# Rounding the first and third matrix of a routed expert on GpSimd instead of loading their rounded copies

## The chip, the cores and the metric

The kernel runs on one core of one Trainium2 chip. The metric is the device time of one execution, in microseconds (us), as a median of several runs.

## The reference

The reference is a small network on 2048 tokens of width 512: a mixture of four experts chosen by token id, a feed-forward block with Hadamard rotations, a WKV recurrence, and last a routed mixture of experts. Only the last part matters here:

```
scores = softmax(xf @ gate_w);  sel = top_k(scores + expert_bias, 2)
routed_in = xf[token_idx] * top_scores_sorted[:, None]        # sorted by expert
h = silu(ragged_dot(routed_in, w1, counts)) * ragged_dot(routed_in, w3, counts)
routed_out = ragged_dot(h, w2, counts)
out = silu(xf @ sw1) * (xf @ sw3) @ sw2                       # shared expert
out = out.at[token_idx].add(routed_out)
```

There are eight routed experts. Each has w1 and w3 of 512 x 448 and w2 of 448 x 512. With the inputs of the reference the experts get 275, 166, 897, 2048, 311, 197, 202 and 0 rows.

## The kernel before, in words

Each float32 product is made of three products of rounded numbers (type float32r): the low part of the activation with the high part of the weight, high with low, and high with high. So each weight matrix must stand in SBUF twice: as Wh, its rounded copy, and as Wl, the raw weight minus Wh.

The work of the last layer goes in tiles of 128 rows, numbered t. Tiles 0 to 15 belong to the shared expert and tiles 16 to 54 to the routed ones. With 128 rows to a tile and at least one tile for each expert, routed expert e0 has tiles 16 to 18, e1 19 and 20, e2 21 to 28, e3 29 to 44, e4 45 to 47, e5 48 and 49, e6 50 and 51, and e7 52 to 54 (it has no rows, and the tiles that are left fall to it).

TensorE takes the routed tiles in one fixed order, in the loop behind L1298. In each turn it transposes the input of tile t+1 (`d_x`, L1282), makes the two up products of tile t (`d_up`, L1311, 24 matmuls), transposes the hidden rows of tile t-1 (`d_mid`, L1330), and makes the down product of tile t-2 (`d_down`, L1346, 12 matmuls). `d_up` of an expert's first tile waits on `s_w13` for both parts of its w1 and w3; `d_down` waits on `s_w2`.

The weights lie in two slots, and expert e uses slot e mod 2. GpSimd (POOL) fills them, with `w_all(idx, slot, ups, downs)`, where idx is e+1. It works in program order:

- It waits until TensorE has done the last up product that reads the slot (`s_dup` at `ups`), which is that of the last tile of expert e-2.
- `w_high` (L585) starts a DMA that casts a raw matrix from HBM straight into Wh. It is issued for w1 (p = 0) and w3 (p = 1), one behind the other.
- `w_low` (L592) waits for the raw matrix in the staging buffer `wst[p]` and for Wh, subtracts one from the other into Wl, and waits for its own end.
- `w_raw` (L576) starts the load of the next expert's raw matrix into `wst[p]`, which is free then.
- Then it waits for the last down product that reads the slot (`s_dd` at `downs`), and does the same for w2 (p = 2).

`alone` (L572) is an addition of one column on GpSimd, put ahead of many of these instructions for every idx above 2. The pair of calls at L742 and L743 runs twice in a hardware loop (experts e2 to e5), and two more calls follow behind it. Expert e0 (idx 1) is loaded by other code that the change leaves as it is.

Ahead of the routed tiles GpSimd issues 32 scatters (L732) of the sorted rows to DRAM. SyncE (SP) waits for their landing and then loads the tiles' inputs into `xsd` (L479, `load`), stores each tile's result (L483, `store`), and fetches the shared expert's rows into `row` (L503). VectorE adds those rows to `xres` on every second tile (L1877), which has two inputs in SBUF. At the end GpSimd gathers the routed results (L754 and L761), VectorE adds them, and SyncE writes the output.

Of the kernel before, what the change touches and what calls it, by code (L numbers as in the profile page):

```python
# [4 lines left out]
ALU = mybir.AluOpType  # L5
# [7 lines left out]
D = 512  # L13
# [29 lines left out]
HID = 448  # L43
# [28 lines left out]
def program(nc, x, tok, ctx, g_xattn, g_ffn, su_ug, su_dp, wscale_ug, wscale_dp, w_up, w_gate, w_down,  # L72
            wkv_w, wkv_u, gate_w, w1, w2, w3, sw1, sw2, sw3, expert_bias, consts, out):
    es = ExitStack()
    with es:
        def sem(name):
            return es.enter_context(nc.semaphore(name))
# [11 lines left out]
        def keep(name, shape, dt=F32):  # L89
            t = nc.alloc_sbuf_tensor_at(name, shape, dt, offset=top[0])  # L90
            size = 4
            for n in shape[1:]:
                size *= n
            top[0] += (size + 31) // 32 * 32
            return t
# [5 lines left out]
        slot = keep("slot", [P, TT], I32)  # L101
# [93 lines left out]
        Wh, Wl = W[:, :, 0, :], W[:, :, 1, :]  # L195
# [117 lines left out]

        s_wst = [sem(f"s_wst{i}") for i in range(3)]
        s_whi = [sem(f"s_whi{i}") for i in range(3)]
        s_w13 = sem("s_w13")
        s_w2 = sem("s_w2")
        s_dxn = sem("s_dxn")
# [4 lines left out]
        s_dup = sem("s_dup")  # L323
# [5 lines left out]
        s_dd = sem("s_dd")  # L329
# [37 lines left out]
        def f32(ap):  # L367
            return ap.bitcast(F32)
# [8 lines left out]
        def w_rows(p, width, at=None):  # L377
            q, step = ((P, G_W), (P, HID), (HP, D))[p]
            return wst[p if at is None else at][0:q, 0:HC * step].rearrange("p (k n) -> p k n", k=HC)[:, :, 0:width]
# [135 lines left out]
        def _(pool):  # L515
# [42 lines left out]
            def w_part(idx, p):  # L558

                if isinstance(idx, int) and idx == 0:  # L560
                    return shared_part[p]
                w, q = ((w1, P), (w3, P), (w2, HP))[p]
                return w[bass.ds(idx - 1, 1), :, :].rearrange("e (k p) n -> p (e k) n", p=q)
# [3 lines left out]
            def alone(idx):  # L567


                if not isinstance(idx, int) or idx > 2:  # L570
                    n = places[0] = places[0] + 1
                    pool.tensor_tensor(pace[:, n:n + 1], pace[:, 0:1], pace[:, 0:1], ALU.add)  # L572

            def w_raw(idx, p):

                pool.dma_start(w_rows(p, (HID, HID, D)[p]), w_part(idx, p)).then_inc(s_wst[p], 16)  # L576

            def w_place(whole, slot, p, width):

                q, at, step = ((P, W_1, G_W), (P, W_3, HID), (HP, W_2, D))[p]  # L580
                return whole[0:q, slot, at:at + HC * step].rearrange("p (k n) -> p k n", k=HC)[:, :, 0:width]

            def w_high(idx, p, slot):

                pool.dma_start(w_place(Wh, slot, p, (HID, HID, D)[p]), w_part(idx, p)).then_inc(s_whi[p], 16)  # L585

            def w_low(idx, p, slot):

                width = (HID, HID, D)[p]
                pool.wait_ge(s_wst[p], 16 * idx)  # L590
                pool.wait_ge(s_whi[p], 16 * (idx + 1))
                pool.tensor_tensor(w_place(Wl, slot, p, width), w_rows(p, width), f32(w_place(Wh, slot, p, width)), ALU.subtract)\  # L592
                    .then_inc((s_w13, s_w13, s_w2)[p], 1)
                if p < 2:
                    pool.wait_ge(s_w13, 2 * idx + p + 1)
                else:
                    pool.wait_ge(s_w2, idx + 1)
# [26 lines left out]
                else:  # L624
                    pool.wait_ge(s_w2, 1)

            def w_all(idx, slot, ups=None, downs=None, more=True):


                if ups is not None:  # L630
                    pool.wait_ge(s_dup, ups)
                    alone(idx)
                for p in range(2):
                    w_high(idx, p, slot)
                for p in range(2):
                    w_low(idx, p, slot)
                    if more:
                        alone(idx)
                        w_raw(idx + 1, p)
                if downs is not None:  # L640
                    pool.wait_ge(s_dd, downs)
                    alone(idx)
                w_high(idx, 2, slot)
                w_low(idx, 2, slot)
                if more:
                    alone(idx)
                    w_raw(idx + 1, 2)
# [80 lines left out]
            for t in range(TT):  # L728
                for k in range(2):
# [3 lines left out]
                                            rows_at[n % 8], None).then_inc(s_rsc[n % 8], 16)  # L733

            w_all(2, 1, TT, TT)

            def w_next(idx, slot, more=True):
                last = pool.value_load(tend1_i[0:1, bass.ds(idx - 3, 1)], min_val=1, max_val=NT1)
                w_all(idx, slot, last + TT, last + TT, more)
# [1199 lines left out]
```

## Time and profile before

| | us |
|---|---|
| median of 3 runs | 1395.21 |
| lowest and highest | 1388.55 and 1401.52 |
| the profiled execution | 1396.1 |
| its span, first to last instruction | 1394.4 |

The mean granted clock of TensorE in the profiled execution is 0.959 of full speed. Instants below are microseconds from the start of the span. In rows of instructions, "x8" counts instructions, and the bracket is the idle time of the engine ahead of them with what ended it.

### The profile page before, as it was taken

What the parts mean: (1) busy time and instruction counts of PE and PEld (TensorE: products, weight loads), DVE (VectorE), ACT (ScalarE), POOL (GpSimd) and SP (SyncE); (2) the same over time, 40 slices, a digit from 0 to 9 for tenths busy, and PEclk for the clock granted to TensorE, in tenths of its full rate; (3) what the DMA queues carried; (4) which work ended last, traced back from release to release, by engine and by line L of the source; (5) the groups of instructions that cost most, each with busy time, mean ns of one, the idle gap of its engine ahead of it and who ended that gap; (6) DMA issues with size and microseconds to landing.
All of it is one profiled execution on the core that took longest, in us unless ns stands there. A gap on an engine that the chain in (4) does not pass through costs nothing.

```text
span 1394.4 us, 18292 instructions
## 1 busy us (share of the span) xinstructions
PE 1271.6 (91%) x6256; PEld 1073.6 (77%) x6257; DVE 652.2 (47%) x1103; ACT 446.7 (32%) x755; POOL 391.7 (28%) x327
## 2 busy tenths in 40 slices
PE   4999899999999999999999889995899999998670
PEld 3888778887888888888888778884788888887560
DVE  6555356644366646674555575563123222222116
ACT  3333342333245323531343457421122222221110
POOL 2221111000022302221334231446454310035554
PEclk9999999999999999999999999998899999999785
DMA  6821456544669845965964030435777552257647
GB/s 204 263 84 54 145 210 243 211 159 191 246 216 349 302 181 202 366 239 196 310 226 156 26 84 31 155 117 206 198 222 230 168 141 75 75 181 220 167 145 254
DMA packets 99035, 259.69 MB, mean 186 GB/s; under 512 B 8636, under 2 KB 42648, under 8 KB 86680
## 3 DMA queue, kind: packets, MB, share of 16 engines
q1 hardware_dynamic: 64824, 160.19, 32.4%
q0 software_dynamic: 33680, 98.35, 23.4%
q8 instruction: 41, 0.67, 0.2%
q10 hardware_dynamic: 464, 0.27, 0.1%
q14 instruction: 26, 0.21, 0.0%
HBM read 183.02 MB, written 75.76 MB: 186 GB/s over the span
## 4 chain that ended last, share of the span: by engine, by line
PE 63%; issue 14%; POOL 10%; DMA 7%; DVE 4%; another core or an unknown queue 1%; ACT 1%; POOLq 0%; ACTq 0%; DVEq 0%
PE bank L1145 25%; PE bank L1173 12%; POOL W L592 6%; PE bank L1311 6%; DMA W<-in_L_ffn_w 5%; PE bank L1070 4%; PE bank L1090 4%; PE bank L1346 2%; PE bank L1100 2%; POOL xs_sorted L732 2%; POOL fin_high L761 1%; PE bank L1117 1%; PE bank L1112 1%; DMA wdn<-in_L_ffn_W_down 1%
## 5 line engine op out<-in xcount | busy, mean ns | idle before, releaser
L1145 PE MATMUL bank<-xTh,G 128*128 128x512 f32 x1024 | 279.4, 398 | 1.8 <-DVE xTl L1592 1.8
L1145 PEld LDWEIGHTS bank<-xTh,G 128*128 128x128 f32 x1024 | 189.4, 189 | 42.8 <-issue 3.4
L1311 PE MATMUL bank<-W,dxh 128*128 (+2 forms) x880 | 204.9, 376 | 0.0
L1311 PEld LDWEIGHTS bank<-W,dxh 128*128 128x128 f32 x880 | 171.8, 195 | 15.9
L1173 PE MATMUL bank<-DN,bhh 128*128 128x512 f32 x512 | 157.9, 390 | 0.0
L1311 PE MATMUL bank<-W,dxl 128*128 (+2 forms) x440 | 117.4, 390 | 32.4 <-POOL W L592 16.4
L1145 PE MATMUL bank<-xTl,G 128*128 128x512 f32 x512 | 138.1, 392 | 0.0
L1746 DVE TENSOR_TENSOR dmid<-bank,dsg 128x448 f32<-128x448 f32 x55 | 34.3, 623 | 203.0 <-ACT dsg L954 194.7
L592 POOL TENSOR_TENSOR W<-wst,W 128x1792 fp32r<-128x1792 f32 (+1 forms) x24 | 101.4, 4226 | 87.7 <-DMA W<-in_L_ffn_w 86.3
L1614 DVE SCALAR_TENSOR_TENSOR bs<-bank,tab,bs 128x512 f32<-128x512 f32 x64 | 47.5, 743 | 160.8 <-PE bank L1145 160.8
L1346 PE MATMUL bank<-W,dhh 112*128 (+1 forms) x440 | 114.6, 403 | 0.0
L1311 PEld LDWEIGHTS bank<-W,dxl 128*128 128x128 f32 x440 | 82.5, 197 | 41.3 <-issue 33.8
L1145 PEld LDWEIGHTS bank<-xTl,G 128*128 128x128 f32 x512 | 96.7, 189 | 20.9
L1173 PEld LDWEIGHTS bank<-DN,bhh 128*128 128x128 f32 x512 | 96.2, 188 | 21.3 <-issue 1.7
L954 ACT ACTIVATE dsg<-bank 128x448 f32<-128x448 f32 x55 | 29.9, 544 | 244.0 <-PE bank L1311 235.2
L1173 PE MATMUL bank<-DN,bhl 128*128 128x512 f32 x256 | 103.8, 405 | 0.0
L1346 PEld LDWEIGHTS bank<-W,dhh 112*128 112x128 f32 x440 | 85.3, 194 | 20.4
L842 ACT ACTIVATE bhh<-bs 128x512 fp32r<-128x512 f32 x64 | 40.3, 629 | 185.4 <-DVE bs L1614 185.4
L1738 DVE TENSOR_TENSOR dxl<-bank,dxh 128x512 fp32r<-128x512 f32 x55 | 37.9, 688 | 115.8 <-ACT dxh L936 115.8
L836 ACT ACTIVATE bs<-bank,tab 128x512 f32<-128x512 f32 x64 | 44.1, 689 | 137.7 <-PE bank L1145 137.7
L522 POOL TENSOR_TENSOR rstd<-vare,cst 128x4 f32<-128x4 f32 x12 | 12.4, 1031 | 228.9 <-DVE vare L1507 228.9
L964 ACT ACTIVATE dys<-bank 128x512 f32<-128x512 f32 x55 | 32.9, 598 | 125.1 <-PE bank L1346 104.0
(247 smaller groups left out, 1961.6 us busy)
## 6 DMA issues: line engine op xcount, KB each, us to landing
G<-gate_up_split SPq DMA_DIRECT2D x48, 1024.0 KB, 7.0
DN<-down_split SPq DMA_DIRECT2D x24, 1024.0 KB, 5.0
wst<-in_L_ffn_w POOLq DMA_DIRECT2D x24, 896.0 KB, 6.2
W<-in_L_ffn_w POOLq DMA_DIRECT2D x24, 896.0 KB, 7.6
gate_up_split<-G SPq DMA_DIRECT2D x16, 1024.0 KB
y_all<-dys SPq DMA_DIRECT2D x55, 256.0 KB
xs_sorted<-zero POOLq DMA_DIRECT2D x3, 3328.0 KB, 21.1
xsd<-xs_sorted SPq DMA_DIRECT2D x39, 256.0 KB, 3.3
```

The lines of the kernel that those rows point to most:

```text
L592: pool.tensor_tensor(w_place(Wl, slot, p, width), w_rows(p, width), f32(w_place(Wh, slot, p, width)), ALU.subtract)\
L836: act.activation(bs[g % 2][:, :], bank[0][:, :], ACT.Silu, scale=tab[:, T_WGT + g % NK:T_WGT + g % NK + 1]).then_inc(s_bs, 1)
L842: act.activation(bhh[g % 2][:, :], bs[g % 2][:, :], ACT.Copy).then_inc(s_bhh, 1)
L1070: mm = pe.matmul(bank[2 + t % 2][:, :], a[t % 2][:, k, :], w[:, bass.ds(ex * DC + k, 1), :], start=(n == 0), stop=(n == 3 * DC - 1))
L1090: mm = pe.matmul(bank[4 + t % 2][:, :], a[t % 2][:, k, :], w[:, bass.ds(ey * DC + k, 1), :], start=(n == 0), stop=(n == 3 * DC - 1))
L1145: mm = pe.matmul(bank[m][:, :], G[:, c % 2, f, h, m, i, :], a[b % 2][:, i, :], start=(n == 0), stop=(n == 3 * DC - 1))
L1173: mm = pe.matmul(bank[2 + i][:, :], a[g % 2][:, i * P:(i + 1) * P], DN[:, c % 2, f, h, :], start=(k == 0 and n == 0), stop=(k == NK - 1 an ...
L1311: mm = pe.matmul(bank[o][:, 0:width], a[par][:, k, :], w[:, bass.ds(slot, 1), at + k * step:at + k * step + width].rearrange("p a n -> p ( ...
L1346: mm = pe.matmul(bank[4][:, :], a[par][:, k, :], w[0:HP, bass.ds(slot, 1), W_2 + k * D:W_2 + (k + 1) * D].rearrange("p a n -> p (a n)"), s ...
L1614: dve.scalar_tensor_tensor(out=bs[g % 2][:, :], in0=bank[1][:, :], scalar=tab[:, T_WUP + g % NK:T_WUP + g % NK + 1], in1=bs[g % 2][:, :], ...
L1738: dve.tensor_tensor(dxl[t % 2][:, :, :].rearrange("p k n -> p (k n)"), bank[0][:, :], f32(dxh[t % 2][:, :, :]).rearrange("p k n -> p (k n) ...
L1746: dve.tensor_tensor(dmid[t % 2][:, :], bank[3][:, 0:HID], dsg[:, :], ALU.mult).then_inc(s_dmid, 1)
```

## The change

GpSimd makes the rounded copies of w1 and w2 itself. For the experts from e1 on, `w_cut` waits for the raw matrix in `wst[p]`, runs one `alone`, copies the matrix with `tensor_copy` into Wh (float32 to float32r), and waits for the copy's end on a new semaphore, `s_wcut`. `w_low_of` is `w_low` without the two waits ahead. `w_all` now takes the order: DMA of w3's rounded copy; copy of w1, subtraction of w1, load of the next raw w1; subtraction of w3, load of the next raw w3; wait for the down products; copy of w2, subtraction of w2, load of the next raw w2. The same holds for all seven calls of `w_all`.

```diff
+            def w_cut(idx, p, slot):
+                width = (HID, HID, D)[p]
+                pool.wait_ge(s_wst[p], 16 * idx)
+                alone(idx)
+                pool.tensor_copy(w_place(Wh, slot, p, width), w_rows(p, width)).then_inc(s_wcut, 1)
+                pool.wait_ge(s_wcut, 2 * idx - 3 + p // 2)
+
+            def w_low_of(idx, p, slot):
+                width = (HID, HID, D)[p]
+                pool.tensor_tensor(w_place(Wl, slot, p, width), w_rows(p, width), f32(w_place(Wh, slot, p, width)), ALU.subtract)\
+                    .then_inc((s_w13, s_w13, s_w2)[p], 1)
+                if p < 2:
+                    pool.wait_ge(s_w13, 2 * idx + p + 1)
+                else:
+                    pool.wait_ge(s_w2, idx + 1)
+
+            def w_all(idx, slot, ups, downs, more=True):
+                pool.wait_ge(s_dup, ups)
+                alone(idx)
+                w_high(idx, 1, slot)
+                w_cut(idx, 0, slot)
+                w_low_of(idx, 0, slot)
+                if more:
                     alone(idx)
-                for p in range(2):
-                    w_high(idx, p, slot)
-                for p in range(2):
-                    w_low(idx, p, slot)
-                    if more:
-                        alone(idx)
-                        w_raw(idx + 1, p)
-                if downs is not None:
-                    pool.wait_ge(s_dd, downs)
+                    w_raw(idx + 1, 0)
+                w_low(idx, 1, slot)
+                if more:
                     alone(idx)
-                w_high(idx, 2, slot)
-                w_low(idx, 2, slot)
+                    w_raw(idx + 1, 1)
+                pool.wait_ge(s_dd, downs)
+                alone(idx)
+                w_cut(idx, 2, slot)
+                w_low_of(idx, 2, slot)
                 if more:
                     alone(idx)
                     w_raw(idx + 1, 2)
```

## Rows read from the trace of the kernel before

**Rows 1.** The page, part 1: busy time, share and instructions of each engine.

```profile
PE 1271.6 (91%) x6256; PEld 1073.6 (77%) x6257; DVE 652.2 (47%) x1103; ACT 446.7 (32%) x755; POOL 391.7 (28%) x327
```

**Rows 2.** Windows of the routed tiles: us, busy per engine, clock, DMA share, GB/s.

```profile
964.00:979.00 15.00, 0.97 (x5) 0.48 (x5) 0.00 (x0) 0.60 (x1) 8.83 (x9) 0.69 0.83 269
...
1128.00:1233.00 105.00, 105.00 (x541) 92.51 (x540) 26.94 (x42) 25.48 (x49) 1.52 (x3) 1.00 0.27 86
...
1300.00:1327.00 27.00, 15.95 (x70) 13.66 (x69) 3.13 (x5) 3.16 (x7) 15.21 (x9) 0.75 0.61 155
```

**Rows 3.** Waits of PE from 960 on: us, times, longest.

```profile
PE bank L1311 <- POOL W L592: 16.4, 2, 11.0
PE bank L1282 <- issue: 14.0, 1, 14.0
```

**Rows 4.** Timeline of PE around tiles 49 to 52.

```profile
1271.09 0.60 PE L1282 MATMUL bank<-cst,xsd 128*128 128x128 f32 x4
...
1279.66 0.60 PE L1282 MATMUL bank<-cst,xsd 128*128 128x128 f32 x4
1285.65 1.85 PE L1311 MATMUL bank<-W,dxl 128*128 x4 [5.39 <-POOL W L592]
...
1316.30 1.86 PE L1311 MATMUL bank<-W,dxl 128*128 x4 [11.05 <-POOL W L592]
```

**Rows 5.** Timeline of POOL while it loads e5, e6 and e7.

```profile
1253.41 0.18 POOL L572 TENSOR_TENSOR pace<-pace 128x1 f32<-128x1 f32 x1 [3.12 <-PE bank L1346]
...
1268.02 0.19 POOL L572 TENSOR_TENSOR pace<-pace 128x1 f32<-128x1 f32 x1
1268.70 1.53 POOL L585 DMA_DIRECT2D W<-in_L_ffn_w  x2 [0.49 <-issue]
1275.95 4.05 POOL L592 TENSOR_TENSOR W<-wst,W 128x1792 fp32r<-128x1792 f32 x1 [5.72 <-DMA W<-in_L_ffn_w]
...
1281.48 3.97 POOL L592 TENSOR_TENSOR W<-wst,W 128x1792 fp32r<-128x1792 f32 x1
...
1294.63 4.63 POOL L592 TENSOR_TENSOR W<-wst,W 112x2048 fp32r<-112x2048 f32 x1 [7.30 <-DMA W<-in_L_ffn_w]
...
1300.21 0.21 POOL L572 TENSOR_TENSOR pace<-pace 128x1 f32<-128x1 f32 x1
```

**Rows 6.** Groups of POOL by form: count, busy us, mean ns, idle before.

```profile
L592 POOL TENSOR_TENSOR W<-wst,W 128x1792 fp32r<-128x1792 f32 x16 | 64.5, 4034 | 36.1 <-DMA W<-in_L_ffn_w 34.7 <-DMA wst<-in_L_ffn_w 1.1
L592 POOL TENSOR_TENSOR W<-wst,W 112x2048 fp32r<-112x2048 f32 x8 | 36.9, 4610 | 51.7 <-DMA W<-in_L_ffn_w 51.6
...
L661 POOL TENSOR_SCALAR ce<-cd,wlim 128x512 f32<-128x512 f32 x16 | 25.1, 1570 | 103.7 <-DVE cd L1639 102.8 <-POOL W L592 0.9
...
L669 POOL TENSOR_TENSOR cev<-cnum,ce 128x512 f32<-128x512 f32 x14 | 18.1, 1296 | 35.6 <-issue 27.3 <-DVE ce L1658 8.3
...
L528 POOL TENSOR_TENSOR nmr<-negm,rstd 128x4 f32<-128x4 f32 x8 | 1.6, 203 | 0.6
...
L517 POOL MEMSET zero<- 128x128 f32 x1 | 0.2, 205 | 3.0 <-DMA cst<-shape_constants 3.0
L700 POOL MEMSET pace<- 128x32 f32 x1 | 0.1, 125 | 0.0
```

**Rows 7.** Instructions on xsd: landing of the loads issued at 972, then of all.

```profile
DMA to landing us min/median/max: 6.6/7.2/7.8
...
DMA to landing us min/median/max: 2.6/3.3/7.8
```

**Rows 8.** Timeline of PE: input of tile 18, eight up matmuls of tile 17 and of tile 18.

```profile
992.21 0.65 PE L1282 MATMUL bank<-cst,xsd 128*128 128x128 f32 x4 [2.45 <-DMA xsd<-xs_sorted]
...
994.51 2.97 PE L1311 MATMUL bank<-W,dxh 128*128 x8
...
1002.41 1.79 PE L1311 MATMUL bank<-W,dxh 128*128 x8
```

**Rows 9.** L1877 on VectorE, durations from 1000 on, min/median/max.

```profile
L1877 DVE SCALAR_TENSOR_TENSOR xres<-row,gates,xres x16: 742/744/3871, 1016.9 to 1278.3; 128x512 f32<-128x512 f32 x16
```

More of the change, by code:

```diff
@@ L315, in program @@
         s_whi = [sem(f"s_whi{i}") for i in range(3)]
+        s_wcut = sem("s_wcut")
         s_w13 = sem("s_w13")
@@ L625, in shared_low @@
                     pool.wait_ge(s_w2, 1)
-            def w_all(idx, slot, ups=None, downs=None, more=True):
-                if ups is not None:
-                    pool.wait_ge(s_dup, ups)
-                    alone(idx)
-                for p in range(2):
-                    w_high(idx, p, slot)
-                for p in range(2):
-                    w_low(idx, p, slot)
-                    if more:
-                        alone(idx)
-                        w_raw(idx + 1, p)
-                if downs is not None:
-                    pool.wait_ge(s_dd, downs)
-                    alone(idx)
-                w_high(idx, 2, slot)
-                w_low(idx, 2, slot)
+            def w_cut(idx, p, slot):
[19 more added lines that the diff above has]
+                if more:
+                    alone(idx)
+                    w_raw(idx + 1, 0)
+                w_low(idx, 1, slot)
+                if more:
+                    alone(idx)
+                    w_raw(idx + 1, 1)
[3 more added lines that the diff above has]
+                w_low_of(idx, 2, slot)
                 if more:
```

## The prediction

> **What bounds the kernel now.** I read the page first. TensorE is busy for 91% of the span [rows 1], so a change off TensorE can only win what TensorE loses to waits. The change touches the routed tiles alone, so the windows of that stage come next. Between 1128 and 1233 us, while e3's 16 tiles run, TensorE is busy for all 105 us at full clock and GpSimd for 1.5 us [rows 2]: nothing about the weights is worth anything there. From 1300 to 1327 it is busy for only 16 of 27 us, at 0.75 of the clock, and GpSimd for 15 [rows 2]. The list of TensorE's waits gives the price: two waits on the subtractions of L592, 16.4 us in all, and one of 14.0 us ahead of tile 16's transposes [rows 3]. The timeline puts the two: 5.39 us ahead of tile 50, the first of e6, and 11.05 us ahead of tile 52, the first of e7 [rows 4]. e5 and e6 have two tiles each, and a tile takes 1279.66 - 1271.09 = 8.57 us [rows 4], while GpSimd takes 1300.21 - 1268.02 = 32.2 us for one expert [rows 5]. That is the bound here: GpSimd's round per expert against 17.1 us of tiles.
>
> In GpSimd's round for e6, 5.72 us go in a wait for the two cast DMAs and 7.30 us in the wait for w2's [rows 5]. Over the run, L592 stands idle 34.7 + 51.6 us for such DMAs [rows 6], but only the rounds of e6 and e7 are on the path.
>
> **What a copy costs.** The trace has no `tensor_copy` on GpSimd, so I bound it per column. The product of L669 takes 1.296 us for 512 columns and that of L528 0.203 us for 4, which is 2.15 ns a column over some 0.2 us; L592 gives (4.034 - 0.203) / 1788 = 2.14 [rows 6]. So the rate holds to 1792 columns, and writing float32r costs nothing extra. That is two reads and one write. A memset, one write, rises from 0.125 us at 32 columns to 0.205 at 128: 0.83 ns a column [rows 6]. A copy has one read and one write. By the memset it would take 1.7 us for w1 and 1.9 us for w2; by L592 4.0 and 4.6 us. The dearest row with one large input is L661, 2.69 ns a column [rows 6], which gives 5.0 and 5.7 us. I take 1.2 ns, nearer the memset, since one read and one write can overlap where two reads seem to add: C = 2.3 us for w1 and D = 2.7 us for w2. The ends 1.7/1.9 and 5.0/5.7 go into the range.
>
> The Trainium skill, GPSIMD Engine Reference, section Engine selection, says that on GpSimd an operation with one input runs at roughly line rate, where one with two inputs is about twice as slow as VectorE. At its 1.2 GHz that would be an estimate of 1.5 us for 1792 columns over the fixed cost, near the lower end; L661, with one large input at 2.69 ns a column [rows 6], speaks against reading the rule for every such operation. By the rule the sum would win some 1 us more.
>
> **GpSimd's round, new.** From its start (the wait on the slot's last up product passed) to w3's subtraction done:
> - first pace instruction to the DMA's issue 0.7, one issue of the pair's 1.53, so 0.77 [rows 5]; second pace and gaps 0.6
> - the copy C, its own wait 0.1
> - subtraction of w1 4.05; to the next subtraction 1281.48 - 1280.00 = 1.5 (a pace and a raw load); subtraction of w3 4.0 [rows 5].
> That is 11.8 + C = 14.1 us, against 17.4 now (1268.02 to 1285.45) [rows 5]. For e7 nothing more is loaded, so 1.4 goes: 10.4 + C = 12.7. The w2 part, from the last down product that reads the slot: two paces and gaps 0.9, D, 0.1, 4.6, so 5.6 + D = 8.3 us. The load of the next raw w2 ends it with 1.2 (1299.26 to 1300.21 is 0.95, and where the loop turns it is more) [rows 5]. Issues, paces and waits are counted in these, and every one of them is on GpSimd's own path.
>
> **The chain at the end.** In the unshifted clock of the trace:
> - e5's w2 may start at 1253.4, after tile 44's down product [rows 5]: done 1261.7, raw load issued 1262.9. Tile 47's up product is long done.
> - e6's w3 is done at 1262.9 + 14.1 = 1277.0. TensorE wants it at 1280.1, just after the transposes of 1279.66 [rows 4]. The wait of 5.39 goes, and so do some 2 us of half clock behind it.
> - Raw load until 1278.2. Now e6's w2 is late by something new: slot 1 is read by tile 47's down product until 1279.7 [rows 4]. Then w2 is done at 1288.0, the raw load at 1289.2.
> - e7's w3 is done at 1289.2 + 12.7 = 1301.9. TensorE is ready for tile 52 at 1280.1 + 2 x 8.57 = 1297.2, and so still waits, 4.7 us. In short, tile 52 starts at 1296.9 + C + D.
> Now it starts at 1316.30 [rows 4]. So the tail wins 14.4 us. What follows (three tiles, the gathers, the additions, the output) hangs on TensorE and moves with it. The copies themselves cost nothing before e6: those of e1 to e5 lie under tiles that run without a gap [rows 2]. Closest is e2: its round begins after tile 18 and tile 21 comes some 20.8 us later, against 14.1 needed.
>
> With L592's rate for the copies GpSimd no longer waits for tile 47, and tile 52 starts at 1290.4 + 2C + 2D = 1307.6: 8.7 us won. With L661's rate it is 1311.8: 4.5 won. With the memset's it is 1300.5: 15.8 won.
>
> **The start of the stage.** Two cast DMAs are issued right behind the scatters, and the inputs of tiles 16 and 17 are loaded at 972, behind them. They land after 6.6 and 7.8 us; the median of all such loads is 3.3 [rows 7]. TensorE waits 14.0 us there [rows 3], with the DMA engines 83% busy at 269 GB/s [rows 2]. One of the two DMAs, 0.92 MB, goes: at 269 GB/s that is at most 3.4 us; I take 2. Tile 18's input makes TensorE wait 2.45 us, and the eight matmuls behind take 2.97 us in place of 1.79 [rows 8]. The cast DMA of w2, which the code puts in the same stretch, goes as well. That is worth 0 to 4; I take 1. From there TensorE and the waits of GpSimd on it move together, so these 3 us (0 to 7) reach the end.
>
> **Sum.** 14.4 + 3 = 17.4 us off the profiled execution's 1396.1 (span 1394.4 and 1.7 around it) gives 1378.7. That execution lies 0.9 above the median, so my forecast for the median is 1378.
>
> **The rivals.**
> - The copy runs at the rate of L592 or L661. For it: L661 has one large input and is dearer than a product with two [rows 6]. Against it: a scalar from memory is part of L661. The gain is 8.7 + 3 or 4.5 + 3, and the time 1384 to 1388.
> - The gain is given back through VectorE. L1877 takes 742 ns, but up to 3871 [rows 9], which is about when a subtraction of GpSimd runs; SyncE waits for it before it fetches the next input. GpSimd's reading time per expert rises from 12.7 to 17.7 us, and some of the 16 additions meet it. If three more do and each holds TensorE up by 1.2 us, and the start wins nothing, 11 us are left: 1384. The Trainium skill, SBUF — State Buffer, section Who interferes with whom, states that a VectorE instruction with two SBUF inputs contends with a GpSimd instruction that reads SBUF, and that the second waits for the first to end; the trace's 3871 ns agrees. By it the copy is a new holder, while the cast DMA never was one.
> - w3's DMA ends last. In e7's round its subtraction could start 8.7 us in. The DMA is issued at 0.7, and e6's first one is there 1275.95 - 1268.70 = 7.25 us after its issue [rows 5]: at 8.0, with 0.7 to spare. Each us more costs one; at 3 us more the time is 1380.
> - Slower: rounding is software on GpSimd, and the copy costs more than any row. Tile 52 starts later than now once 1290.4 + 2C + 2D passes 1316.3, that is from 3.3 ns a column on. At 4.5 ns (8.3 and 9.4 us) it starts at 1325.8, 9.5 later; with the 3 us won at the start the time is 1402. Against it: the subtraction rounds too, at no price [rows 6].
>
> **How the numbers follow.** A measurement of this kernel tells about 1% from no change. That bound lies at 1381.3 below and 1409 above. The forecast has 0.62 and its own times run from 1373 to 1383, most of it under the bound; the copy at the dearer rates 0.20; VectorE or w3's DMA together 0.12; slower than before 0.06, little of that over 1409. Faster by over 1%: 0.55. Within 1%: 0.42. Slower by over 1%: 0.03. The range is 1371 (the memset's rate and the start's full 7 us) to 1388 (L661's rate).
>
> **What would show it.** Right: `tensor_copy` on GpSimd at 2 to 3 us; TensorE's waits on the subtractions down from two to one of some 5 us, ahead of tile 52; no wait ahead of tile 50; GpSimd waiting for tile 47's down product in e6's round; its waits on W's DMA gone but for moments; the 14.0 us ahead of tile 16 down to 12. The forecast is wrong if the copies take 4 us or more, if tile 52 still starts over 10 us late, or if xsd waits grow.

## The result and the profile after

The changed kernel takes 1375.12 us, the median of 4 runs (1371.3 to 1377.29), against 1393.39 us for the kernel before (4 runs). The medians lie 18.3 us apart; the ratio of the two, as the comparison estimates it, is 0.9857 with a 95% interval of 0.9821 to 0.9893, which is 19.9 us. On another chip, beside other runs, the same two kernels gave 1371.77 and 1385.98 us, ratio 0.9898 (0.9882 to 0.9915), 14.1 us. The forecast was 17.4, and 1378 us for the median.

The page of the changed kernel, part 1, answers to [rows 1]. GpSimd is busier by 15 us and has 12 more instructions: the copies add 25.1 us, and 14 issues of a DMA at some 0.77 us each are gone:

```profile
PE 1265.0 (92%) x6256; PEld 1069.8 (78%) x6257; DVE 652.6 (48%) x1103; ACT 446.4 (33%) x755; POOL 407.0 (30%) x339
```

TensorE's waits from 960 us on answer to [rows 3]. Of 16.4 us in two waits on the subtractions, 3.7 in one are left, and the wait ahead of tile 16 is 12.2 in place of 14.0:

```profile
PE bank L1300 <- issue: 12.2, 1, 12.2
PE bank L1364 <- issue: 5.4, 1, 5.4
PE bank L1329 <- POOL W L593: 3.7, 1, 3.7
PE bank L1300 <- DMA xsd<-xs_sorted: 2.2, 4, 1.3
```

The groups of GpSimd by form answer to [rows 6]: count, busy us, mean ns, then the idle time before. The copies are there as CAST, seven of each size, at 1.694 and 1.888 us. The subtraction of w3, which alone still waits for a casting DMA, has 5.8 us of idle time left; [rows 6] had 34.7 and 51.6:

```profile
L593 POOL TENSOR_TENSOR W<-wst,W 128x1792 fp32r<-128x1792 f32 x9 | 36.3, 4033 | 7.1 <-DMA W<-in_L_ffn_w 5.8 <-DMA wst<-in_L_ffn_w 1.3
...
L638 POOL TENSOR_TENSOR W<-wst,W 112x2048 fp32r<-112x2048 f32 x7 | 33.1, 4726 | 0.6
...
L633 POOL CAST W<-wst 112x2048 fp32r<-112x2048 f32 x7 | 13.2, 1888 | 0.5 <-PE bank L1364 0.5
...
L633 POOL CAST W<-wst 128x1792 fp32r<-128x1792 f32 x7 | 11.9, 1694 | 0.0
```

The timeline of GpSimd from the start of e6's round answers to [rows 5]:

```profile
1249.93 0.20 POOL L573 TENSOR_TENSOR pace<-pace 128x1 f32<-128x1 f32 x1
1250.27 0.77 POOL L586 DMA_DIRECT2D W<-in_L_ffn_w  x1
...
1251.19 1.69 POOL L633 CAST W<-wst 128x1792 fp32r<-128x1792 f32 x1
1252.96 4.06 POOL L638 TENSOR_TENSOR W<-wst,W 128x1792 fp32r<-128x1792 f32 x1
...
1260.09 4.00 POOL L593 TENSOR_TENSOR W<-wst,W 128x1792 fp32r<-128x1792 f32 x1 [2.07 <-DMA W<-in_L_ffn_w]
...
1272.84 0.33 POOL L573 TENSOR_TENSOR pace<-pace 128x1 f32<-128x1 f32 x2 [7.77 <-PE bank L1364]
1273.11 1.89 POOL L633 CAST W<-wst 112x2048 fp32r<-112x2048 f32 x1
...
1279.91 0.74 POOL L577 DMA_DIRECT2D wst<-in_L_ffn_w  x1
...
1280.88 0.77 POOL L586 DMA_DIRECT2D W<-in_L_ffn_w  x1
...
1290.34 3.96 POOL L593 TENSOR_TENSOR W<-wst,W 128x1792 fp32r<-128x1792 f32 x1 [2.70 <-DMA W<-in_L_ffn_w]
```

The wait of 7.77 us for tile 47's down product is the new link that the prediction named. From there to the end of e7's w3, GpSimd needs 1294.30 - 1272.84 = 21.5 us, 2.70 of them a wait for w3's own DMA. The timeline of TensorE answers to [rows 4]:

```profile
1250.12 1.06 PE L1329 MATMUL bank<-W,dxl 128*128 x4
...
1259.81 0.65 PE L1300 MATMUL bank<-cst,xsd 128*128 128x128 f32 x4 [1.31 <-DMA xsd<-xs_sorted]
1261.71 1.85 PE L1329 MATMUL bank<-W,dxl 128*128 x4 [1.25 <-issue]
1263.37 3.19 PE L1329 MATMUL bank<-W,dxh 128*128 x8
...
1272.94 1.06 PE L1329 MATMUL bank<-W,dxl 128*128 x4
...
1294.50 1.54 PE L1329 MATMUL bank<-W,dxl 128*128 x4 [3.71 <-POOL W L593]
```

Tile 50 (1272.94) no longer waits for weights. But tile 49 starts 1261.71 - 1250.12 = 11.6 us after tile 48 in place of 8.57. The transposes of tile 50's input waited 1.31 us for its load, the product behind them 1.25 more, and then eight matmuls took 3.19 us in place of 1.79. Tile 50 follows after 11.2 us. That is 3.0 + 2.7 = 5.7 us that the forecast did not have. A window over that stretch gives the granted clock, the third value from the right:

```profile
1261.70:1267.00 5.30, 5.29 (x14) 4.73 (x15) 0.12 (x1) 0.00 (x0) 3.29 (x3) 0.50 0.52 169
```

It is 0.50, the lower of TensorE's two levels (1.2 and 2.4 GHz), and it fell after the idle 1.31 and 1.25 us.

**Where the 22.3 us between the two profiled spans lie.** I measured every run from the end of the last scatter, where the first changed instruction stands, and cut what follows at the starts of tiles 19 and 52 (first product of `d_up`). All columns are differences of instants in the timelines, in us. The last column is the part of "19 to 52" that lies between the starts of tiles 48 and 52; four tiles without any wait would take 4 x 8.57 = 34.3 us.

```
run                    last scatter ends   to tile 19   19 to 52   52 to the end    48 to 52
before                 970.35              39.7         306.2      78.1             53.4
before, again          962.92              35.5         310.0      77.9             53.6
changed                964.35              35.4         294.7      77.6             44.4
changed, again         961.95              36.8         297.3      76.9             42.4
e1 w1 only             959.97              40.4         299.6      77.0             48.2
e2 w2 only             964.55              38.1         299.0      76.5             45.4
e3 all three           963.91              32.9         287.4      77.6             37.1
e3 again               965.07              32.0         287.5      77.8             37.1
e4 copy twice          962.81              37.6         290.4      77.2             40.9
e5 first round old     961.81              38.2         294.2      77.5             38.7
e6 DMAs kept           962.69              35.3         299.4      76.8             45.1
e7 raw w2 behind       964.31              36.8         293.8      76.8             41.9
e8 up weights first    970.17              31.9         284.1      76.1             34.3
e9 input first         968.95              35.1         288.2      77.5             39.0
```

Of the 22.3 us, 6.0 lie ahead of anything changed, 4.3 before tile 19, 11.5 between tiles 19 and 52, and 0.5 behind. The first 6.0 are chance: the kernel before, profiled again, ends its scatters at 962.92, and a changed one (e8) at 970.17. Of the 11.5 us between tiles 19 and 52, 9.0 lie between tiles 48 and 52. The other 2.5 lie between tiles 19 and 48, where TensorE waits for no weights in either kernel; that stretch takes from 249.2 to 256.4 us over the fourteen profiles, and the second profile of the kernel before has the longest.

### The profile page after: what moved, and what is told of

Same layout as the page of the kernel before. It is cut to its first block, busy times and chain, and to the rows that moved or that the text cites. A ratio compares the mean times of both kernels' runs of the same rounds, so it can differ in the third digit from the quotient of the medians.

```text
span 1372.1 us, 18291 instructions
## 1 busy us (share of the span) xinstructions
PE 1265.0 (92%) x6256; PEld 1069.8 (78%) x6257; DVE 652.6 (48%) x1103; ACT 446.4 (33%) x755; POOL 407.0 (30%) x339
## 4 chain that ended last, share of the span: by engine, by line
PE 84%; DVE 4%; DMA 4%; issue 3%; POOL 2%; ACT 1%; another core or an unknown queue 1%; SPq 0%; ACTq 0%; POOLq 0%; DVEq 0%
PE bank L1163 26%; PE bank L1329 18%; PE bank L1191 12%; PE bank L1364 10%; PE bank L1088 4%; PE bank L1108 4%; PE bank L1118 2%; PE bank L1300 2%; PE bank L1348 1%; DMA xsd<-xs_sorted 1%; PE bank L1135 1%; DMA fin_high<-y_all,slr 1%; PE bank L1074 1%; DVE wl L1504 1%
## 5 line engine op out<-in xcount | busy, mean ns | idle before, releaser
L1329 PE MATMUL bank<-W,dxh 128*128 (+2 forms) x880 | 202.1, 372 | 0.0
L1329 PEld LDWEIGHTS bank<-W,dxh 128*128 128x128 f32 x880 | 169.0, 192 | 15.4
L1329 PE MATMUL bank<-W,dxl 128*128 (+2 forms) x440 | 115.1, 384 | 19.9 <-DVE dmid L1764 9.1
L1764 DVE TENSOR_TENSOR dmid<-bank,dsg 128x448 f32<-128x448 f32 x55 | 34.3, 624 | 186.6 <-ACT dsg L972 186.6
L1163 PEld LDWEIGHTS bank<-xTl,G 128*128 128x128 f32 x512 | 96.1, 188 | 20.8
L982 ACT ACTIVATE dys<-bank 128x512 f32<-128x512 f32 x55 | 32.9, 598 | 123.0 <-PE bank L1364 105.9
L1364 PE MATMUL bank<-W,dhl 112*128 (+1 forms) x220 | 66.2, 423 | 6.3 <-issue 5.4
## 6 DMA issues: line engine op xcount, KB each, us to landing
xs_sorted<-zero POOLq DMA_DIRECT2D x3, 3328.0 KB, 20.8
```

The costliest lines, as they stand in the source:

```text
L982: act.activation(dys[t % 2][:, :], bank[4][:, :], ACT.Copy).then_inc(s_dy, 1)
L1163: mm = pe.matmul(bank[m][:, :], G[:, c % 2, f, h, m, i, :], a[b % 2][:, i, :], start=(n == 0), stop=(n == 3 * DC - 1))
L1329: mm = pe.matmul(bank[o][:, 0:width], a[par][:, k, :], w[:, bass.ds(slot, 1), at + k * step:at + k * step + width].rearrange("p a n -> p ( ...
L1364: mm = pe.matmul(bank[4][:, :], a[par][:, k, :], w[0:HP, bass.ds(slot, 1), W_2 + k * D:W_2 + (k + 1) * D].rearrange("p a n -> p (a n)"), s ...
L1764: dve.tensor_tensor(dmid[t % 2][:, :], bank[3][:, 0:HID], dsg[:, :], ALU.mult).then_inc(s_dmid, 1)
```

## The experiments

**The kernel before and the changed one, once more.** No edit.

> The kernel before, profiled again on this chip. In its first profile the last scatter ended at 970.35 us, where every later profile has it at 960 to 964, though nothing ahead of it is changed; and the stage behind it took 424.05 us. If that shift is chance, the last scatter ends at 960 to 966 here. Tile 19 at 38 to 40 us after it, the stage at 422 to 425 us, two waits on the subtractions of 5 to 6 and 11 us.

The kernel before gave a ratio of 0.9999 (0.9977 to 1.0021) to itself. Its two waits on the subtractions are 5.56 and 11.44 us, so the tail of the stage is steady (53.4 and 53.6 us between tiles 48 and 52); 19 to 52 took 310.0 us. The start is not: tile 19 comes after 35.5 us, 4.2 earlier than in the first profile, with the same three casting DMAs.

> The changed kernel itself, beside the others on one chip. In its profile the input of tile 50 took 8.3 us to land, while the raw w2 and the rounded w3 were in flight. If that is the rule, TensorE again waits on xsd shortly before tile 49's products; if it was chance of the phase, the wait is absent and tile 52 starts some 3 to 6 us earlier after the last scatter than the 330.1 us of the first profile. Ratio to the kernel before 0.984 to 0.988.

The wait on xsd ahead of tile 49 came again, 1.14 us and 1.06 behind it, and the half clock too. Tile 52 starts at 334.1 us after the scatters, later than in the first profile and not earlier, and the ratio, 0.9898, lies just outside what I expected. So the late input was not a chance of one execution: both profiles of this kernel have it. It does not come every time either, as the profile of e5 shows.

**e1: round only w1 on GpSimd.** The copy of w2 goes back to its casting DMA:

```diff
-                w_cut(idx, 2, slot)
-                w_low_of(idx, 2, slot)
+                w_high(idx, 2, slot)
+                w_low(idx, 2, slot)
```

> Only w1 is rounded on GpSimd; the rounded copies of w2 and w3 are loaded by casting DMAs. Theory (GpSimd's round is the price): from tile 47's down product to e6's w2 done takes 12 to 13 us as in the kernel before, not the 6.9 of the changed kernel, so tile 52 starts some 6 us later than in the changed kernel, and the time is about 1381. Rival (only the DMA traffic counts, and w2's DMA runs while nothing else is in flight): no later than the changed kernel by more than 2 us, 1375 to 1377.

1379.5 us, ratio 0.9935 (0.9909 to 0.996). The timeline of GpSimd shows w2 of e6 and w3 of e7:

```profile
1271.30 0.72 POOL L586 DMA_DIRECT2D W<-in_L_ffn_w  x1
1280.57 4.61 POOL L593 TENSOR_TENSOR W<-wst,W 112x2048 fp32r<-112x2048 f32 x1 [8.55 <-DMA W<-in_L_ffn_w]
...
1295.84 3.95 POOL L593 TENSOR_TENSOR W<-wst,W 128x1792 fp32r<-128x1792 f32 x1 [2.66 <-DMA W<-in_L_ffn_w]
```

w2's part takes 13.9 us, 1271.30 to 1285.18, where I expected 12 to 13, and tile 52 waits 12.56 us. GpSimd starts that part 2.6 us after tile 47's down product is done, held by its own work alone, and tile 52 comes 31.3 us after that product, against 21.8 and 21.2 in the two profiles of the changed kernel: later by 9.5 us or more, where I expected 6. GpSimd's round is the price, as the theory has it. The changed kernel was not run on the chip of e1 to e4, so they are compared with it by their ratios. That of 0.9935 stands against 0.9857 and 0.9898, so w2's copy is worth between a third and somewhat over a half of the gain.

**e2: round only w2 on GpSimd.** w1 and w3 come by a pair of casting DMAs again, as in the kernel before.

> Only w2 is rounded on GpSimd; w1 and w3 come by a pair of casting DMAs. Theory (GpSimd's round): e7's round to the end of w3's subtraction takes 15.9 us as before in place of 13.7, so tile 52 starts 2 to 3 us later than in the changed kernel, and the start of the stage loses part of its 4 us, since two casting DMAs run beside the first inputs again: about 1380. Rival (the wait for w3's own DMA is what ends last, so w1's copy brings nothing at e7): tile 52 not later by more than 1 us and the time within 1 us of the changed kernel where the start is left out.

1379.32 us, ratio 0.9927 (0.9906 to 0.9948). In e7's round the pair's first DMA makes the subtraction wait 6.55 us, tile 52 waits 8.04 us, and 19 to 52 takes 3.0 us more than the changed kernel's mean of 296.0. Tile 52 comes 26.5 us after tile 47's down product, some 5 us later than in the changed kernel, where the theory had 2 to 3; its direction holds, its size was too small, and the rival falls. The copies alone bring 0.65% (e1) and 0.73% (e2), and the two together 1.4% in one comparison and 1.0% in the other. By the first the gains add up, by the second they overlap; these runs do not decide it.

**e3: round all three.** No casting DMA is left in the seven rounds.

```diff
-                w_high(idx, 1, slot)
                 w_cut(idx, 0, slot)
                 w_low_of(idx, 0, slot)
...
-                w_low(idx, 1, slot)
+                w_cut(idx, 1, slot)
+                w_low_of(idx, 1, slot)
```

> GpSimd rounds w3 too, so no casting DMA is left in these rounds. Theory (w3's DMA both ends last in the rounds of e6 and e7 and, beside the raw load of w2, makes the input of tile 50 late by 8.3 us from issue): e7's round to w3 done falls from 13.7 to about 12.2 us, the wait on xsd ahead of tile 49's products and the half clock behind it go (5.7 us), and the time is about 1368. Rival (VectorE's addition or chance made that input late): the wait on xsd stays, and the time is 1373 to 1375. Second rival (GpSimd's longer reading time collides with VectorE's additions): waits on xsd grow, 1377 or more.

1362.05 us, ratio 0.9799 (0.9777 to 0.9822): 25.7 us below the kernel before on that chip by the medians, 27.9 by the ratio, and 6 us below what the theory had. In TensorE's waits there is no wait on xsd at all:

```profile
PE bank L1300 <- issue: 10.7, 1, 10.7
PE bank L1329 <- POOL W L638: 2.6, 1, 2.6
PE bank L1329 <- DVE dmid L1764: 1.8, 2, 1.1
```

Tiles 19 to 52 take 287.4 us, 8.6 below the changed kernel's mean (6.3 of them between tiles 48 and 52), and tile 19 comes 3 us earlier. GpSimd's added reading time did not show: L1895, the addition of VectorE, was held up to 3.9 us here, as long as before [rows 9], and TensorE waited for nothing behind it.

**e4: every copy twice.** The second copy writes the same bytes.

```diff
-                pool.tensor_copy(w_place(Wh, slot, p, width), w_rows(p, width)).then_inc(s_wcut, 1)
-                pool.wait_ge(s_wcut, 2 * idx - 3 + p // 2)
+                for again in range(2):
+                    if again:
+                        alone(idx)
+                    pool.tensor_copy(w_place(Wh, slot, p, width), w_rows(p, width)).then_inc(s_wcut, 1)
+                    pool.wait_ge(s_wcut, 4 * idx - 7 + 2 * (p // 2) + again)
```

> Each copy of w1 and w2 is made twice, with a wait and one pace instruction between, so each w_cut is longer by 2.1 us. Theory (w3's DMA ends last in e7's round and hides w1's copy): only w2's second copy shows, tile 52 starts about 2 us later after tile 47's down product, and the time is about 1377. Rival (the sum of the prediction, tile 52 at a fixed time plus both copies): about 4 us later, 1379.

1368.68 us, ratio 0.9852 (0.9832 to 0.9872): no slower than the changed kernel, and 19 to 52 is shorter, 290.4 us. Both expectations missed this. The timelines show two effects. From tile 47's down product to tile 52 it takes 23.9 us against 21.8 and 21.2, so 2.1 to 2.7 more, which is near the theory's 2 and not the rival's 4. (GpSimd does not wait for that product here; it comes to w2 half a us after it, held by its own work.) But GpSimd issues the raw w2 only 0.4 us ahead of the load of tile 50's input and the cast of w3 1.1 us behind it, where the changed kernel issues them 2.2 and 1.2 us ahead, and the load lands after 6.0 us in place of 8.3. TensorE's only wait on xsd is the one at the start of the stage:

```profile
PE bank L1303 <- issue: 12.9, 1, 12.9
PE bank L1332 <- POOL W L593: 6.3, 1, 6.3
PE bank L1303 <- DMA xsd<-xs_sorted: 2.3, 1, 2.3
```

Tiles 48 to 52 take 40.9 us in place of 44.4 and 42.4. A slower GpSimd moved its two DMAs out of the way of the input's load, and in this profile that was worth more than the 2.1 to 2.7 us.

**e5: the first round as before.** e1's weights come with three casting DMAs at the start of the stage; the other six rounds are as changed.

```diff
+                w_high(idx, 0, slot) if first else None
                 w_high(idx, 1, slot)
-                w_cut(idx, 0, slot)
-                w_low_of(idx, 0, slot)
+                if first:
+                    w_low(idx, 0, slot)
+                else:
+                    w_cut(idx, 0, slot)
+                    w_low_of(idx, 0, slot)
...
-            w_all(2, 1, TT, TT)
+            w_all(2, 1, TT, TT, first=True)
```

> The first round (expert e1, at the start of the stage) is done as in the kernel before, with three casting DMAs; the other six rounds as changed. Theory (the start of the stage wins about 4 us from the DMAs that are gone): tile 19 starts 39 to 41 us after the last scatter, as before (39.7), in place of 35.4 to 37.6, and the time is 3 to 4 us above the changed kernel. Rival (that gain was chance, xsd waits there being the scatters' and not the casts'): tile 19 at 35 to 38 us, and the same time as the changed kernel within 1 us.

1370.65 us, ratio 0.9889 (0.9872 to 0.9905), against 1371.77 and 0.9898 for the changed kernel on the same chip. Tile 19 comes after 38.2 us, 1.4 later than there; the time is the same. The theory's 4 us are not there. Over all runs, tile 19 comes after 39.7, 35.5, 38.2 and 38.1 us with two casts ahead (before twice, e5, e2), a mean of 37.9, and after 35.4, 36.8, 37.6, 36.8 and 35.1 with the changed order (changed twice, e4, e7, e9), a mean of 36.3. With no cast at all it is 32.9, 32.0 and 31.9. So the change wins some 1.5 us there, within the spread of the runs, and only the last cast brings more. Two profiles fit neither group and speak against reading much into the 1.5: e1, with w3's cast ahead and w2's behind it, has 40.4, the latest of all, and e6, with the casts of w1 and w2 going to DRAM, has 35.3.

This profile shows something else. From the second round on its code is that of the changed kernel, yet TensorE does not wait for tile 50's input:

```profile
1263.69 0.60 PE L1308 MATMUL bank<-cst,xsd 128*128 128x128 f32 x4
1264.46 1.08 PE L1337 MATMUL bank<-W,dxl 128*128 x4 [0.18 <-issue]
```

The load lands after 6.4 us in place of 8.3 and 8.1. GpSimd issued the raw w2 and the cast of w3 3.9 and 2.2 us ahead of it, not 2.2 and 1.2, after TensorE had waited 0.48 us for tile 48's input and 0.53 behind it. Tiles 48 to 52 take 38.7 us. So the late input depends on how the issues of the two engines happen to lie, and no run here shows how often it comes.

**e6: keep the DMAs, drop the waits.** The casts of w1 and w2 are issued as before, into a buffer in DRAM that nobody reads:

```diff
+            def w_spare(idx, p):
+                q = (P, P, HP)[p]
+                there = spare_dram[bass.ds(idx * 3 + p, 1), 0:q, :, 0:(HID, HID, D)[p]].rearrange("a p k n -> p (a k) n")
+                pool.dma_start(there, w_part(idx, p)).then_inc(s_whi[p], 16)
...
+                w_spare(idx, 0)
                 w_high(idx, 1, slot)
...
+                w_spare(idx, 2)
                 w_cut(idx, 2, slot)
```

> As the changed kernel, but the casting DMAs of w1 and w2 are issued as well where they stood before, into a spare buffer in DRAM that nothing reads and nobody waits for. It keeps the traffic and the two issues of 0.8 us, and takes the waits away. Theory (the waits on GpSimd's path are most of the gain, the traffic some 4 us at the start and up to 6 at tile 50): the ratio to before is 0.989 to 0.994, that is 6 to 10 us worse than changed: issues 1.6 us per round at the end, start 3 to 4 us, w3's DMA later by 2 to 3 us in e7's round. Rival (traffic is free, only waits count): not more than 3 us above the changed kernel. Rival (traffic is all): no gain over the kernel before.

1380.22 us, ratio 0.9968 (0.995 to 0.9987), 8.4 us above the changed kernel beside it, inside the theory's 6 to 10: by time most of the gain is gone. GpSimd no longer waits for the casts of w1 and w2, but its wait for w3's cast grew, to 3.79 us in e7's round from 2.70 and 2.15, and the extra issues lie on its path. The profiled execution was the fastest of five (1375.7), so it shows too little of this; there, tile 52 waits 6.7 us, and tiles 48 to 52 take 45.1 us, 1.7 above the changed kernel's mean of 43.4 and 8.4 below the mean before. The rival "traffic is free" falls. "Traffic is all" falls by that profile, and by time only by the edge of the interval. The run does not divide its loss between the traffic and the issues. A caution: these casts end in DRAM and not in SBUF, so their price need not be that of the DMAs removed.

**e7: the raw w2 load behind w3's cast.**

```diff
                 w_high(idx, 1, slot)
+                if not isinstance(idx, int) or idx > 2:
+                    w_raw(idx, 2)
                 w_cut(idx, 0, slot)
...
                 w_low_of(idx, 2, slot)
-                if more:
-                    alone(idx)
-                    w_raw(idx + 1, 2)
```

> The raw load of an expert's w2 is moved from the end of the round before to just behind the casting DMA of w3, from e2 on. Theory (the raw load that is issued 1 us ahead of w3's DMA makes that one land after 9.4 us): w3's DMA lands in about 7 to 8 us, GpSimd's wait of 2.7 us in e7's round shrinks to under 1.2, and tile 52 starts 1 to 2 us earlier after tile 47's down product (21.7 us in the changed kernel). Rival (the two share the engines whatever the order): the wait stays at 2 to 3 us and, the issue now being on the path, the time is the same or up to 1 us above.

1368.56 us, ratio 0.9878 (0.9862 to 0.9895). w3's subtraction no longer waits for its DMA in the rounds of e6 and e7, and tile 52 follows tile 47's down product after 19.9 us in place of 21.2 in the changed kernel beside it. So the order of the two issues decides which lands first. The two still share the DMA engines: the raw w2, now second, lands after 10.3 and 9.6 us. And the inputs are late more often:

```profile
PE bank L1299 <- issue: 13.2, 1, 13.2
PE bank L1299 <- DMA xsd<-xs_sorted: 6.0, 5, 2.7
PE bank L1328 <- issue: 1.8, 4, 0.5
PE bank L1328 <- POOL W L593: 1.6, 2, 1.1
```

By time it is no different from the changed kernel: the intervals overlap.

**e9: SyncE loads the input before the row.**

```diff
             for t in range(TT + 2, TT + NT1 - 2):
+                load(t + 2)
                 if t % 2 == 0 and t <= TT + 2 * TT:
                     wait(sp, s_sha, (t - TT - 2) // 2)
                     sp.dma_start(row[:, 0, :], ...).then_inc(s_shl, 16)
-                load(t + 2)
```

> The changed kernel with SyncE loading the next tile's input before it fetches the row for VectorE's addition, so that the input waits neither for VectorE nor behind the row. Theory (the raw w2 and the rounded w3 in flight make the input of tile 50 late): the wait on xsd ahead of tile 49 stays at 0.7 us or more, since the two DMAs are issued at 1249 to 1250, ahead of it either way. Rival (the row and VectorE's addition make it late): the wait goes, and the time is 3 to 5 us below the changed kernel, ratio about 0.986 where that one has 0.990.

1368.85 us, ratio 0.9835 (0.9803 to 0.9868), and my theory did not hold as I put it: the wait on xsd ahead of tile 49 is gone. TensorE's waits:

```profile
PE bank L1300 <- issue: 13.7, 1, 13.7
PE bank L1364 <- issue: 3.9, 1, 3.9
PE bank L1329 <- POOL W L593: 3.4, 1, 3.4
PE bank L1329 <- issue: 1.4, 3, 0.5
PE bank L1300 <- DMA xsd<-xs_sorted: 0.8, 1, 0.8
```

Yet the load is still slow. Here are the issues of GpSimd and SyncE around it:

```profile
1252.33 0.73 POOL L577 DMA_DIRECT2D wst<-in_L_ffn_w  x1
...
1253.40 0.77 POOL L586 DMA_DIRECT2D W<-in_L_ffn_w  x1
...
1254.10 0.43 SPq L480 DMA_DIRECT2D xsd<-xs_sorted  x1
...
1254.57 0.47 SPq L505 DMA_DIRECT2D row<-y_all  x1
```

It lands after 7.5 us, against 8.1 in the changed kernel run again and a median of 3.0 of all. There it is issued behind the row, 0.5 us later against the store before it. So the two DMAs of GpSimd make the load slow, and the row ahead of it takes the rest of its slack: about 1 us in all. With the waits and the half clock behind them that 1 us is worth 3 to 5: from tile 48 to tile 50 it takes 18.2 us here and 22.8 and 21.4 in the two profiles of the changed kernel. VectorE has no part in it: its addition took 0.74 us at that place, and SyncE did not wait for it.

**e3 again, and e8: the next expert's w1 and w3 before the present w2.** e8 rounds all three on GpSimd and splits each round in two:

```diff
+            w_up(2, 1, TT)
+            w_down(2, 1, TT)
+            w_up(3, 0, used(3))
+            with pool.Fori(3, E1 - 2, 2) as idx:
+                w_up(idx + 1, 1, used(idx + 1))
+                w_down(idx, 0, used(idx))
+                w_up(idx + 2, 0, used(idx + 2))
+                w_down(idx + 1, 1, used(idx + 1))
+            w_up(E1, 1, used(E1), False)
+            w_down(E1 - 1, 0, used(E1 - 1))
+            w_down(E1, 1, used(E1), False)
```

> GpSimd rounds all three matrices, a second time, beside the others of this chip. Ratio to the kernel before 0.978 to 0.983; no wait on xsd ahead of tile 49; tile 19 at 33 us after the last scatter if the absent casting DMA is what makes the start shorter, 35 to 38 if it was chance.

> All three matrices rounded on GpSimd, and the order of the rounds changed: w1 and w3 of the next expert are prepared before w2 of the present one, so that e7's w1 and w3 no longer wait behind tile 47's down product. Theory (that wait is what still ends last ahead of tile 52): tile 52 wants its weights some 317.5 us after the last scatter and has them at about 314; the wait of 2.6 us and 1.5 us of half clock behind it go, and the time is 3 to 5 us below the kernel that rounds all three. Rival (GpSimd's own work is the bound, whatever the order): tile 52 or a down product behind it still waits 2 us or more, same time within 1 us.

e3 gave 1364.19 us and 0.9813 (0.978 to 0.9847) this time; e8 gave 1361.53 us and 0.9786 (0.9759 to 0.9812). In the profile the wait ahead of tile 52 is gone and 19 to 52 takes 284.1 us, 3.4 below e3. By time, e8 is 2.7 us below e3 with intervals that overlap. e8 is the fastest version here, 30 us below the kernel before. Its chain no longer holds tile 47's down product; one wait of 0.8 us on w2 of e6 is what is left of the weights:

```profile
1291.20 0.60 PE L1353 MATMUL bank<-cst,dmid 128*112 128x128 f32 x4
1292.59 1.19 PE L1369 MATMUL bank<-W,dhl 112*128 x4 [0.79 <-POOL W L641]
```

## Why the prediction was right

**The bound.** Right. GpSimd's round per expert against two tiles per expert set the end of the stage, and the waits ahead of tiles 50 and 52 came again in the second profile of the kernel before. e1 and e2 each put back a part of the round and lost about a third to a half of the gain.

**The price of a copy.** The method of bounds held, the value I took was too high: 1.69 and 1.89 us for 1792 and 2048 columns, where I took 2.3 and 2.7. It is the memset's rate, my lower bound (1.7 and 1.9). The Trainium skill's rule (GPSIMD Engine Reference, section Engine selection), that an operation with one input runs at roughly line rate, agrees: (1.888 - 1.694) / 256 columns is 0.76 ns a column. L661's 2.69 ns [rows 6] is then no guide to a copy. The rival with dear copies and the slower one both fall.

**The chain at the end.** The prediction's term was 14.4 us; with the measured copies it would have been 15.8. It was reckoned with everything up to tile 48 held still, so the last column of the table answers to it: 53.4 and 53.6 us before, 44.4 and 42.4 after, a gain of 9.0 and 11.2, in the mean 10.1. This term was too large by 4.3 us. Two things are missing from it, and both were steps that it named and set at nothing or gave small odds:
- w3's DMA. I had it land 0.7 us before it was wanted; it landed 2.70 us (2.15 in the second profile) after, since the raw w2 load is issued 1 us ahead of it. e7 takes that wait away.
- The input of tile 50. It was late by 1.3 us and cost 5.7 (4.2 in the second profile). My rival for this went through VectorE's addition, and that was wrong: the slow step is the load itself, with GpSimd's two DMAs and the row ahead of it (e9, e4, e3).
Against that, the small pieces of GpSimd's round were shorter than I counted: 21.5 - 2.7 = 18.8 us from tile 47's down product to e7's w3, where the sum with the measured copies has 20.8. Tile 50 itself did not wait for weights, as forecast, and tile 52 waited 3.7 us where I had 4.7. Where the input was in time (e5) the stretch takes 38.7 us, beside 53.4 - 14.4 = 39.0 in the forecast. That this is so close is luck: the copies and the small pieces were priced too high by some 3.4 us, and w3's DMA, 2.3 us late there, had been priced at nothing.

**The start of the stage.** This term was mis-sized: 3 us forecast, about 1.5 found, and that within the spread of the runs. The 4.3 us between the first two profiles, which seemed to confirm it, are mostly chance, as the second profile of the kernel before and e5 show; between the second profiles of the two kernels tile 19 comes 1.3 us later, not earlier.

**The sum.** 10.1 in the tail, 2.0 between tiles 19 and 48, 1.5 at the start and 0.7 behind tile 52 give about 14 us, which is the ratio of the second comparison (14.1). The 2.0 and the 0.7 lie where the forecast had nothing, and they and the 1.5 are within what profiles of one kernel differ by. The first comparison, 18.3 us by the medians and 19.9 by the ratio, has chance on its side. So the mechanism was right, and the number is in part luck: the forecast of 17.4 lies between the two comparisons because the dear copies and long pieces made up for some of what the late input and w3's DMA took.

**The signs it named.** One of its signs of being wrong came in one pair of profiles: TensorE's waits on xsd went from 3.1 to 2.2 us in the first and from 2.2 to 4.5 in the second. The copies ended below the 2 to 3 us that it named, and the wait ahead of tile 16 fell to 12.2 as named (15.4 and 13.4 in the second profiles). The lower end of its range, 1371 us, is 1.4 below what its own terms give: 1396.1 - 15.8 - 7 - 0.9 = 1372.4.

## What to carry to other kernels

Where one engine both issues DMAs and waits for them, price its whole round against the work that it must hide under, and look for the shortest stretch of such work: here two tiles of 8.57 us. An elementwise copy on an engine that stands waiting for a casting DMA is cheap, here 1.7 us against a wait of 5 to 7. When a round gets faster, list what it will issue, and beside whose loads: a small load with little slack can then be the next thing late, and issuing that load first, or dropping the big one, can be worth more than the microsecond that it is late by (3 to 5 us in the profile of e9).

## What the runs showed that I had not expected

- Making each copy twice did not make the kernel slower (e4, 0.9852 against 0.9857 and 0.9898): 2.1 to 2.7 us more on the path moved two DMAs back against a load that they had delayed.
- An input that came 1.3 us late cost 5.7 us in all, and the same code lost nothing there in another profile (e5). The idle time of 1.31 + 1.25 us was followed by one stretch at the lower clock, where eight matmuls took 3.19 us in place of 1.79.
- The same code ahead of the stage ends between 960.0 and 970.4 us from one execution to the next, and the start of the stage varies by 4 us with nothing changed. Two single profiles are not enough for a term of that size.
